# First norms, router steps and clock fillers moved in a two-layer transformer kernel on one Trainium2 core

## What is computed

```python
x = x + 0.5 * ffn(layernorm(x))        # 128 -> 512 -> 128, gelu, ternary weights
x = x + attention0(layernorm(x))       # 16 heads of 8: causal softmax, plus a second
                                       # linear-attention path on v[t+1] - y[t]
x = x + 0.5 * ffn(layernorm(x))        # the same weights
x = x + 0.5 * moe(layernorm(x))        # 8 experts, top 1, capacity 256 tokens each
x = x + attention1(layernorm(x))       # linear attention, feature map elu(z)+1
x = x + 0.5 * moe(layernorm(x))
```

## Time and profile before

| | us |
|---|---|
| median of 3 runs | 682.89 |
| the runs | 682.93, 678.61, 682.89 |
| profiled execution | 677.53 |
| its span, which all positions below count from | 675.7 |
| mean granted clock of TensorE | 0.91 |
| busy: TensorE, VectorE, ScalarE, GpSimd | 539.5, 359.3, 197.0, 189.2 |

### The profile page before, as it was taken

How to read it: one execution, slowest core, us unless ns; L and a number is a source line. 1 busy time by engine, 2 the same in 40 slices (tenths; PEclk the granted TensorE clock), 3 DMA queues, 4 the chain that set the end, 5 groups by cost and what they waited for, 6 DMA issues and landing times.

```text
span 675.7 us, 10276 instructions
## 1 busy us (share of the span) xinstructions
PE 539.5 (80%) x3836; PEld 336.0 (50%) x3836; DVE 359.3 (53%) x942; ACT 197.0 (29%) x278; POOL 189.2 (28%) x226
## 2 busy tenths in 40 slices
PE   1787777898999889989879767975697898786893
PEld 1664332444544544453357653862355565553593
DVE  4545664467676856672164451323587866833121
ACT  1445220643245135316513510212231311110120
POOL 8555470011020101102102338452221120303154
PEclk9989775899999999999988877997899988977998
DMA  8227876732432262216299313212747162101220
GB/s 277 96 71 245 261 236 213 171 99 87 102 117 69 98 139 79 62 49 162 64 174 238 105 47 126 72 52 66 203 148 203 53 191 79 48 1 48 94 73 10
DMA packets 73666, 79.85 MB, mean 118 GB/s; under 512 B 10946, under 2 KB 50499, under 8 KB 73360
## 3 DMA queue, kind: packets, MB, share of 16 engines
q1 hardware_dynamic: 71056, 73.61, 39.2%
q0 software_dynamic: 2560, 5.58, 2.4%
HBM read 44.07 MB, written 35.72 MB: 118 GB/s over the span
## 4 chain that ended last, share of the span: by engine, by line
PE 48%; DVE 18%; POOL 9%; issue 9%; DMA 7%; ACT 5%; SPq 2%; POOLq 1%; DVEq 0%; ACTq 0%
PE ps_accum L1395 22%; PE ps_pair L1395 16%; PE ps_turn L1395 6%; POOL xe_scr L585 4%; DVE sb_mpart L1078 2%; DMA sb_ring<-sb_qs 2%; DVE sb_work L1152 2%; POOL sb_rstd L566 2%; PE ps_turn L1403 2%; DVE sb_work L1290 2%; DMA y_scr<-sb_y_tmp,sb_places_back 2%; DVE sb_stats L975 1%; SPq L355 1%; ACT sb_work L826 1%; DMA sb_ka_stk<-mk_scr 1%
## 5 line engine op out<-in xcount | busy, mean ns | idle before, releaser
L826 ACT ACTIVATE sb_work<-ps_pair 128x1024 f32<-128x1024 f32 x80 | 80.2, 1026 | 50.2 <-PE ps_pair L1395 49.3
L1395 PE MATMUL ps_pair<-sb_ring,sb_xsets 128*128 128x512 f32 x160 | 64.3, 478 | 10.5 <-DMA sb_ring<-sb_qs 5.0
L1078 DVE TENSOR_REDUCE sb_mpart<-ps_turn 128x4 f32<-128x512 f32 x80 | 55.0, 687 | 30.9 <-PE ps_turn L1395 30.8
L1078 DVE TENSOR_REDUCE sb_mpart<-ps_accum 128x4 f32<-128x512 f32 x80 | 55.1, 688 | 21.3 <-PE ps_accum L1395 20.6
L1395 PE MATMUL ps_accum<-sb_work,sb_v_aug 128*32 128x128 f32 (+3 forms) x768 | 57.9, 396 | 0.3 <-ACT sb_work L826 0.3
L1395 PE MATMUL ps_turn<-sb_ring,sb_m_sets 128*128 128x512 f32 x80 | 41.5, 518 | 9.2 <-DVE sb_mpart L1078 9.2
L1395 PE MATMUL ps_accum<-sb_ring,sb_m_sets 128*128 128x512 f32 x80 | 44.5, 556 | 4.1 <-DVE sb_mpart L1078 3.8
L1395 PE MATMUL ps_pair<-sb_ident_bf,sb_ones_bf 128*128 128x512 bf16 x130 | 37.9, 452 | 11.7 <-DMA sb_x<-y_scr 7.9
L646 POOL TENSOR_TENSOR sb_e_pad<-sb_v_next,sb_y_ar 128x128 f32<-128x128 f32 x16 | 7.4, 460 | 127.3 <-DVE sb_y_ar L1122 127.3
L1395 PEld LDWEIGHTS ps_pair<-sb_ring,sb_xsets 128*128 128x128 f32 x160 | 30.7, 199 | 21.4 <-issue 9.0
L564 POOL TENSOR_SCALAR sb_ve<-sb_mv 128x4 f32<-128x4 f32 x24 | 5.6, 234 | 123.0 <-DVE sb_mv L978 122.4
(11 more groups left out here) (252 smaller groups left out, 1028.4 us busy)
## 6 DMA issues: line engine op xcount, KB each, us to landing
sb_expert_rows<-xe_scr SPq DMA_DIRECT2D x16, 258.0 KB
sb_m_sets<-q_scr SPq DMA_DIRECT2D x16, 256.0 KB
sb_xsets<-k_scr SPq DMA_DIRECT2D x16, 256.0 KB
sb_ka_stk<-mk_scr SPq DMA_DIRECT2D x4, 1024.0 KB
xe_scr<-sb_cst SPq DMA_DIRECT2D x4, 1024.0 KB, 13.1
sb_mw<-in_mw SPq DMA_DIRECT2D x16, 256.0 KB, 5.7
sb_ka_stk<-mk_scr SPq DMA_DIRECT2D x8, 512.0 KB
q_scr<-sb_qs SPq DMA_DIRECT2D x12, 256.0 KB, 3.5
```

The costliest lines, as they stand in the source:

```text
L826: act.activation(banks[:, 2 * i:2 * i + 2], pair[u % 2][:], ACT.Exp, scale=SCALE).then_inc(s["exp_done"], 1)
L1078: dve.tensor_reduce(mpart[:, m // NPAIR, m % NPAIR, :], max_banks[m % 2][:].rearrange("p (h k) -> p h k", h=HL), AX.X, ALU.max).then_inc(s ...
L1395: return pe.matmul(dst, lhsT, rhs, start=start, stop=stop, skip_group_check=True)
```

## The change

1. *Ring cleared in parts.* The memset of the ring becomes three: half (0, 2) behind the first variance, a quarter (2, 3) behind the bias of batch 1, a quarter (3, 4) behind batch 3's norm, with the memset of `v_aug` behind it.
2. *First sum ahead of batch 3's norm.* On VectorE the addition of output(0) and the moments of batch 0's second norm come before the moments of batch 3's first norm; then batch 0 is normalised, `low(2)` done, and batch 3 normalised. GpSimd's order of variances follows. `low(0)` moves between the two ternarisations, and `hidden(0)` waits only for the first.
3. *Tables.* ScalarE gets 128x1 activations (`ready`) that make it load the next function's table at chosen places: Gelu at the start and behind the features of batch 0, Exp behind the first `max_t`, Gelu behind the first attention, and Gelu behind `router_exp(0)`.
4. *Router steps inside the next output.* `turn_second` and `logits` of the batch before stand behind the second and third quarter of `output(f)`; before, both stood behind `hidden(f + 1)`. VectorE does `choose` between moments and normalise, and the sum and reciprocal of `place` come behind the ranks (with one more wait, `top_rcp`).
5. *Variances between half scatters.* The scatters of batches 0 and 1 are cut in two, with the next variance between the halves.
6. *Fillers.* 12 before the first scores; 13, 4, 2, 4 around the last router steps; 6 to 14, 20 to 27 in the entry of the second attention and 18 to 27 before `turn_exit(3)`.
7. *VectorE's second loop.* `place_exit(b - 1)` stands before `divide(b, 3)`.

```diff
         def norm_first(b):
-            return b + B * (b // B)
+            return (0, 1, 2, 4)[b] if b < B else b + B
         def norm_second(b):
-            return b + B * (b // B) + B
+            return (3, 5, 6, 7)[b] if b < B else b + 2 * B
...
             rsqrt(0)
+            clear_ring(0, 2)
...
+            rsqrt(1, 1)
+            add_bias(1, 1, 0, s["ffn_base"])
+            clear_ring(2, 3)
+            rsqrt(2, 0)
+            add_bias(2, 2, 0, s["ffn_base"])
+            before_attention(0)
+            rsqrt(norm_first(3), norm_first(3) % 2)
+            add_bias(norm_first(3), 3, 0, s["ffn_base"])
+            clear_ring(3, 4)
+            pool.memset(v_aug[:], 0.0).then_inc(s["zeroed"], 1)
...
-            for b in range(B):
+            for b in range(2):
                 rsqrt(norm_second(B + b), b % 2)
-                if b:
-                    scatter(0, b - 1)
-            scatter(0, B - 1)
+            for b in range(2, B):
+                scatter(0, b - 2, 0, 2)
+                rsqrt(norm_second(B + b), b % 2)
+                scatter(0, b - 2, 2, NT)
+            for b in range(B - 2, B):
+                scatter(0, b)
...
+            def ready(function):
+                act.activation(act_ready[:], const("ones")[:, 0:1], function)
...
+                if b == 1:
+                    ready(ACT.Gelu)
...
             max_t(0)
+            ready(ACT.Exp)
...
-                norm(norm_second(B + b), old, rows_out[0][b])
+                moments(norm_second(B + b), old, b % 2)
                 if b:
                     choose(b - 1, accum[1])
+                normalise(norm_second(B + b), old, rows_out[0][b], b % 2)
...
+            ffn_x(0, x[0], x[0][:])
+            moments(norm_second(0), x[0], norm_second(0) % 2)
+            dve.wait_ge(x_loaded[3], 16)
+            moments(norm_first(3), x[3], norm_first(3) % 2)
+            normalise(norm_second(0), x[0], values_of[0], norm_second(0) % 2)
+            low(2)
...
+                if b:
+                    place_exit(b - 1)
                 divide(b, 3)
-                if b:
-                    place_exit(b - 1)
...
+                def route(i):
+                    if i == 1:
+                        if b + 1 < B:
+                            turned_first_read(f + 1)
+                        turn_second(f - 1, rows_out[0][b - 1])
+                    elif i == 2:
+                        if b >= 2:
+                            pe.wait_ge(s["lg_sub"], b - 1)
+                            pe.wait_ge(s["rank_c"], 2 * b - 2)
+                        logits(b - 1, f - 1, accum[1], xnT[(b - 1) % 2])
+                output(f, route if b else None)
...
+            stay_awake(12, pair[1][:, 1])
             pe.wait_ge(s["max_t_evac"], 1)
...
-            stay_awake(18, pair[0][:, 0])
+            stay_awake(27, pair[0][:, 0])
             turn_exit(B - 1)
```

86 lines of the change are left out of this document (45 added, 41 removed).

## The result

The changed kernel took 657.87 us in the median of four executions (657.94, 652.56, 657.8, 662.79) against 680.75 for the kernel before: a ratio of 0.9645, 95% interval 0.9574 to 0.9716. It was measured in two later groups too: 660.14 against 683.88 (0.9667, 0.9584 to 0.975) and 662.12 against 683.06 (0.9741, 0.9689 to 0.9794).

What follows compares the result with a forecast made beforehand. Attention loops and experts were taken as TensorE's own work, front and routers as chains across engines. Terms 4.3 + 1.5 + 3.5 + 0.5 + 1.4 + 2.9 − 0.5 = 13.6, taken as 13: 682.89 − 13 = 670 us, range 661 to 679.

Steps and rivals of the forecast that it cites:

- front: Start of the kernel up to the max-score loop: second output pair and projections early, gain 4.3 us, bounds 2.5 and 5.5.
- start of the attention: First scores and exp: hidden table load 1.28 plus clock 3 minus fillers 2.6; gain 1.5 us, bounds −1 and +3.
- first router: Second feed-forward's router steps: last scatter near 409.5 instead of 414.81; 3.5 net after the experts' loss, bounds 1 and 5.
- first experts: After the first router: TensorE idles some 4.4 us and the first expert may start at low clock, −1.5 (0 to −2.5).
- entry of the second attention: More fillers in the second attention's entry, credited +0.5 us for the clock.
- second loop: Second attention's loop: place_exit ahead of divide, 0.7 us for each of b = 1, 2; 1.4 (−2 to +2).
- exit: Batch 3's exit: earlier variance, full clock, minus fillers and place, gain 2.9; longer idle time before the experts, −0.5.
- the router rival: GpSimd's four scatters a batch set the router's end however TensorE is ordered: 4.8 us less, 675; chance 0.12.
- slower by the clock: Rival: idle TensorE leaves experts(0) at 0.50 clock; one slow expert costs 3.8 us, all eight give 700; chance 0.03.
- The unknown that I had bounded: Front: whether GpSimd's memset holds VectorE's first normalise to 12.6; about 1 us at first output either way, bounds 0 to 2.6.
- The fillers: Attention start, router, second attention: extra TensorE products to keep the clock; before the first scores they cost 2.6, win some 3.
- given back: Rival, whole kernel: parts won but absorbed by memsets, SyncE's queue, fillers and slow experts; about 3.5 us, 679; chance 0.17.

Runs made afterwards that it cites:

- 4.1 alone: The kernel before with only VectorE's second-loop order changed (place_exit ahead of divide): 673.82 us against 682.85 (0.9866).
- the undone order: The changed kernel with VectorE's second loop put back (divide ahead of place_exit again): 668.47 us (ratio 0.9815).
- the hold removed: The changed kernel with the first two parts of the ring's memset cleared ahead of the first variance: 657.63 us.
- before again: The kernel before, unchanged, measured once more with its own profile: 681.20 us (ratio 1.0011).

## Why the prediction was wrong

The direction held, the size did not: 13 forecast, 21 to 24 measured. Against the means of the two profiles of before and the three of the changed kernel, the sum compares so, in us gained:

| part | forecast | measured |
|---|---|---|
| front and start of the attention | 4.3 + 1.5 | 3.7 |
| first attention | 0 | 2.3 |
| first router | 5.0 | 5.7 |
| first experts | −1.5 | −0.6 |
| entry of the second attention | 0.5 | 1.0 |
| second loop | 1.4 | 4.9 |
| exit | 2.9 − 0.5 | 3.0 |
| sum | 13.6 | 20.0 |

The loop is more than half of the 6.4 us that are missing. It is not all: with the 4 us that the order is worth there the forecast would have been 667, inside the range. The 2.3 us of the first attention have no isolated cause. The 3.7 of front and start come with max loops whose clock the change does not set, so how much of them is luck stays open. The range was mis-added too: with the bounds named for front, start and loop and with no slow expert, 13.6 + 1.2 + 1.5 + 0.6 + 1.5 is 18.4, which gives 664.5 and not 661; and the 4.8 us of the router rival stand in no sum, since the stage was credited with 3.5. By the stages:

- **The second loop, between leave(0) and leave(3): this is the term that failed.** I credited 0.7 us each for b = 1 and 2, 1.4 in all, and named −2 to +2 as its bounds. It is 3.6 to 6.5 by the changed kernel's profiles, 4.1 alone, and over all profiles some 2 for each of b = 1 and 2. I set the later turn of the answers (2.1 us) against the earlier scatter and took the loop for TensorE's own work. But the wait of VectorE for the variance (1.47 us in before, 0.32 now) lies on the path: TensorE waits behind it for the masks (1.39 in before, 1.56 in the undone order), and the slower products after that wait count too. The same wait for b = 3 is the exit's.
- **The exit** was right in mechanism and nearly in size: 2.4 forecast (2.9 − 0.5), 3.0 measured. The term for the 27 fillers was real: with 18 it is 3.6 to 3.8. The idle time before experts(1) stayed at 1.86 (1.76 before); my −0.5 for it did not come.
- **The first router.** 59.5 us from the attention's end to the last scatter were forecast (350.0 to 409.5), 58.4 measured. The loss of 1.5 for a cold first expert did not come in this profile: the 32 fillers start at 398.94 and last 9.91 us, not 7.2 as at full clock, so TensorE idles 0.77 and not 4.4 us. Net 6.4 in this profile against 3.5. The danger is real in other profiles. In the third measurement of the changed kernel:

```profile
408.01 0.64 PE L1744 MATMUL ps_turn<-sb_cst,sb_expert_rows 128*128 128x128 f32 x2 [2.04 <-DMA sb_expert_rows<-xe_scr]
409.16 3.78 PE L1428 MATMUL ps_pair<-sb_y_tmp,sb_mw 128*128 128x256 f32 x8 [0.52 <-ACT sb_y_tmp L902]
```

  After 2.04 us idle the eight products take 3.78 us, 1.99 in before and in the changed kernel's first profile, and the stage of the experts is 48.8 us, not 46.5. This happened in 4 of the 20 profiles, with the old router's order too, and in all four TensorE had idled 2.03 to 2.24 us. That is the burst that starts cold, of which the Trainium skill's "TensorE: Matmul & The Clock Gate" (HAM oscillation) speaks; it cost 2.3 us and ended within the stage, so the rival "slower by the clock" had its mechanism and not its length. The idle time does not decide it alone: with VectorE's second loop undone TensorE idled 2.29 us at this place and the eight products took 1.99. And the 0.58 from 114 to 126 us, which I had read as agreeing, shows nothing of the kind: the clock had been 0.50 from 94 us on, before TensorE idled.
- **The front.** 4.3 forecast; none of it is shown. The unknown that I had bounded went to the held side: the memset cost the normalise 3 us (4.09 for 1.12 without it). This agrees with the Trainium skill's "SBUF — State Buffer" (the two separate sides): one of the two engines has the ports for a whole instruction. But that was not the term that failed. I had the splits 2.5 us early, and they were 0.5: the variance of batch 1 stood behind both memsets until 42.50, where 40.53 had been. And with the hold removed and everything 4.7 us earlier, the median did not move. I had counted an early arrival at the max loop as time won.
- **The start of the attention.** 1.5 forecast; from the end of the max loop to the first exp it is 7.9, 7.5 and 6.4 us against 7.5 and 10.3. What is late next when the loop ends early I had not seen: SyncE's load of the next set, which goes out at 109.7 in the changed kernel and in before again and lets the row of maxima leave only at 111.75, 1.3 us after it is there. Nor do the 12 fillers surely buy the clock: here they end at 112.47, TensorE idles 2.32 us for the row, and the first product of the scores takes 0.76 us as in before. In the 11 profiles with them it took 0.47 to 0.78 us, in the 9 without 0.76 or 0.77.
- **The fillers** were booked at about 1 us of gain in several places; none shows in the time. **The tables** were booked at 1.28 for one load; 2 to 8 is measured. The Trainium skill's "ScalarE: Activation LUTs" (What ACT_TABLE_LOAD costs) prices a switch at 2.66 us; the rows show 1.28 with the operation right behind it, and only the totals, which are too wide, would allow more.

The rivals: "given back" (679) holds for the front and the fillers alone. That GpSimd's scatters set the router's end did not hold for the change (the stage gained 5 to 6 us) and is half true of its result: the last eight transfers run one behind the other from 395.12 to 404.93, so TensorE's order can win there only by making the first of them start earlier; GpSimd idles 1.38 us ahead of it.

## What to carry to other kernels

Where TensorE waits for VectorE in each turn of a loop, an idle time of VectorE ahead of the awaited instruction counts whole, and here TensorE paid again in clock: read the wait in one turn, times the turns that have it, before setting gains and losses of neighbours against each other. An order that puts a short step into a known wait of several microseconds was worth 9 us by the medians and 8 by the stages; fillers and an earlier front gave nothing that could be measured. Before a stage's clock is explained or sold as a gain, profile the same kernel twice.
